# Cross-attention of a decoder layer: values of key tiles taken two by two in three of four head pairs, second half of the output projection one slot later

## The reference

```python
x = layernorm(x + attn(x))            # causal attention with squared features, 16 heads of 16
x = layernorm(x + xattn(x, ctx))      # 8 heads of 64:
#   q = x @ Wq ; k = ctx @ Wk ; v = ctx @ Wv
#   out = softmax(q k^T / 8) v ; out @ Wo + bo
x = layernorm(x + ffn(x))             # 8 experts, each token goes to its best 2
```

## Time and profile before

| | us |
|---|---|
| median of the timed runs | 1395.97 |
| the profiled execution's own time | 1389.87 |
| its span, first to last instruction | 1388.1 |
| cross-attention in it | 361 to 1106 |
| TensorE busy over the span | 1204.9 (87%) |
| VectorE / ScalarE / GpSimd busy | 769.4 / 587.1 / 681.5 |

### The profile page before, as it was taken

The page is one execution under the profiler, slowest core; times in us unless marked ns, Lnnn a source line. Parts: engine busy times, 40 slices in busy tenths (PEclk is TensorE's granted clock), DMA queues, the critical chain, the costliest instruction groups (busy, mean ns, idle before and its releaser), DMA issues. The chain is left out here.

```text
span 1388.1 us, 19049 instructions
## 1 busy us (share of the span) xinstructions
PE 1204.9 (87%) x6456; PEld 696.9 (50%) x6456; DVE 769.4 (55%) x1427; ACT 587.1 (42%) x1017; POOL 681.5 (49%) x601
## 2 busy tenths in 40 slices
PE   3567777875899999999999999999999799999990
PEld 3334544543455555555555555555555356666660
DVE  6575768655445574455683466655567343433325
ACT  3446555752344454344544444543544322222222
POOL 0123332442257776577777577685777821311112
PEclk8587989886899999999999999999999899999995
DMA  5490000010000010000010000000003531211104
GB/s 186 158 342 23 2 0 2 1 48 24 1 1 1 1 48 0 1 1 1 25 32 24 0 1 1 25 31 1 1 1 131 202 108 31 76 42 42 43 27 181
DMA packets 33132, 64.83 MB, mean 47 GB/s; under 512 B 4349, under 2 KB 22526, under 8 KB 32768
## 3 DMA queue, kind: packets, MB, share of 16 engines
q1 hardware_dynamic: 23328, 32.41, 7.3%
q10 hardware_dynamic: 6304, 22.76, 5.1%
q0 software_dynamic: 3408, 8.46, 1.7%
HBM read 53.06 MB, written 28.51 MB: 59 GB/s over the span
## 5 line engine op out<-in xcount | busy, mean ns | idle before, releaser
L671 POOL TENSOR_TENSOR acc<-acc,PX 128x1024 f32<-128x1024 f32 (+1 forms) x176 | 418.8, 2379 | 138.5 <-ACT PX L941 132.0
L941 ACT ACTIVATE PX<-PS 128x1024 f32<-128x1024 f32 (+1 forms) x208 | 212.4, 1026 | 269.3 <-PE PS L1759 262.9
L1407 DVE TENSOR_REDUCE mxp<-PS 128x2 f32<-128x804 f32 x256 | 241.8, 988 | 130.9 <-PE PS L1674 130.7
L1770 PE MATMUL PS<-PX,V 128*64 128x512 f32 (+1 forms) x832 | 222.6, 620 | 2.0 <-ACT O_raw L883 1.1
L609 POOL TENSOR_SCALAR_AFFINE_SELECT A<-A 128x128 f32<-128x128 f32 x256 | 85.4, 345 | 215.1 <-ACT A L822 211.8
L1828 PE MATMUL PS<-W,XBT 128*128 x312 | 150.6, 606 | 1.1 <-ACT XBT L973 0.8
L720 POOL DMA_INDIRECT Y<-yb,goal_u x39 | 38.3, 983 | 194.1 <-DVE yb L1473 175.0
L822 ACT ACTIVATE A<-PS 128x512 f32<-128x512 f32 (+3 forms) x256 | 97.3, 443 | 72.5 <-PE PS L1570 66.2
L1570 PE MATMUL PS<-qT,kT 128*128 128x512 f32 (+3 forms) x256 | 81.0, 401 | 36.4 <-ACT A L822 31.3
L1759 PEld LDWEIGHTS PS<-QH,KH 64*128 64x128 f32 (+1 forms) x416 | 38.3, 180 | 145.4 <-issue 87.5
L1759 PE MATMUL PS<-QH,KH 64*128 64x512 f32 (+1 forms) x416 | 102.9, 491 | 2.5 <-ACT PX L941 1.3
(11 more groups left out here) (275 smaller groups left out, 2111.7 us busy)
## 6 DMA issues: line engine op xcount, KB each, us to landing
W<-in_w SPq DMA_DIRECT2D x24, 512.0 KB, 5.1
XB<-XG ACTq DMA_DIRECT2D x39, 130.0 KB, 2.1
yl<-Y SPq DMA_DIRECT2D x8, 512.0 KB, 6.7
X<-in_x SPq DMA_DIRECT2D x1, 2048.0 KB, 12.0
out<-X SPq DMA_DIRECT2D x8, 256.0 KB, 2.1
xt_raw<-in_xt SPq DMA_DIRECT2D x3, 512.0 KB, 4.4
c_raw<-in_ctxt SPq DMA_DIRECT2D x6, 200.0 KB, 2.5
c_raw<-in_ctxt SPq DMA_DIRECT2D x12, 100.0 KB, 2.6
```

What stands on the lines that cost most here:

```text
L671: ins = pool.tensor_tensor(sums[0:r], sums[0:r], PX[0:r, (NL * p + t) % NP, :, :], ALU.add)
L941: act.activation(PX[0:r, u % NP, :, :], PS[0:r, score_buffer(u):score_buffer(u) + 2, :], ACT.Exp, scale=XD ** -0.5)\
L1407: dve.tensor_reduce(mxp[:, p % 2, :, v % NT, v // NT:v // NT + 1].rearrange("p a o -> p (a o)"), PS[:, k:k + 2, 0:BW], AX, ALU.max)\
L1770: mm = pe.matmul(PS[rows, 4, :], V[0:LROWS[j], j, P * p + XD * half:P * p + XD * half + XD], PX[0:LROWS[j], u % NP, half, :], start=(j == ...
```

## The change

For the pairs p = 1, 2, 3 a new table `VALUES_LATER` says in which slot the values of which tiles are taken: tiles 0 and 1 in slot 2, 2 and 3 in slot 4, 4 and 5 in slot 6, 6 and 7 in slot 8, 8 and 9 in slot 10, tile 10 in slot 11. Slots 1, 3, 5, 7 and 9 take none. Tiles 11 and 12 stay in slot 0 of the next pair, and pair 0 stays as it was. For p of 1 or more the second half of `wo` moves from slot 8 to slot 9, and the transposes that stood in slot 9 (`ft` 1 at p = 1, `xt` 0 at p = 2) move to slot 8.

```diff
-        ROUTING = {(1, 6): [("ft", 0)], (1, 9): [("ft", 1)], (1, 10): [("gate",), ("choose", 0)],
+        ROUTING = {(1, 6): [("ft", 0)], (1, 8): [("ft", 1)], (1, 10): [("gate",), ("choose", 0)],
...
-                if j in (7, 8):
-                    steps += [(ob, ("wo", op, j - 7))]
+                if j in (7, 9 if p >= 1 else 8):
+                    steps += [(ob, ("wo", op, 0 if j == 7 else 1))]
...
             if p == PAIRS - 2 and more:
-                steps += {6: [(1, ("xcopy",))], 9: [(1, ("xt", 0))], 10: [(1, ("xt", 1))], 11: [(1, ("ctx", 0))], 12: [(1, ("ctx", 1))]}.get(j, [])
+                steps += {6: [(1, ("xcopy",))], 8: [(1, ("xt", 0))], 10: [(1, ("xt", 1))], 11: [(1, ("ctx", 0))], 12: [(1, ("ctx", 1))]}.get(j, [])
...
+        VALUES_LATER = {2: [0, 1], 4: [2, 3], 6: [4, 5], 8: [6, 7], 10: [8, 9], 11: [10]}
...
+                        elif p >= 1:
+                            for t in VALUES_LATER.get(j, []):
+                                values_t(b, NL * p + t)
                         elif 1 <= j < NL - 1:
                             values_t(b, u - 1)
```

More of the change, by code:

```diff
@@ L310, in decoder_layer @@
                    (3, 9): [("scatter", 0)], (3, 10): [("scatter", 1)], (3, 11): [("scatter", 2)], (3, 12): [("scatter", 3)]}
-        LAST_ROUTING = {(1, 6): [("ft", 0)], (1, 9): [("ft", 1)], (1, 10): [("gate",), ("choose", 0)],
+        LAST_ROUTING = {(1, 6): [("ft", 0)], (1, 8): [("ft", 1)], (1, 10): [("gate",), ("choose", 0)],
                         (1, 11): [("choose", 1)], (1, 12): [("choose", 2)], (2, 0): [("choose", 3), ("choose", 4)],
```

## The result

| | before | changed |
|---|---|---|
| median of 16 runs each, us | 1396.44 (1392.26 to 1400.58) | 1390.43 (1384.48 to 1395.59) |
| ratio of the runs, 95% interval | | 0.996 (0.9946 to 0.9975) |
| profiled execution, us | 1389.87 | 1389.92 |
| its span, us | 1388.1 | 1388.0 |
| first transpose of the experts, us | 1105.82 | 1104.95 |

The change makes the kernel faster by 0.4%, 6.0 us of the medians; 1390.4 us was forecast. But the two profiled executions are equally long. The execution of before that was profiled was faster than all 16 timed ones, and the one of the changed kernel had bad luck in one place, which the second experiment shows. A single pair of traces gives a wrong answer on the sum here, and the right one on the parts.

A forecast was written before the change was run, and what follows sets the result against it. TensorE's own sequence of starts was taken as the bound. Terms -7.2 + 0.8 + 0.6 + 0.2 + 0.9 + 0.7 - 1.6 = -5.6 us took the median from 1395.97 to 1390.4 us, range 1383 to 1398.

The forecast's parts named there:

- the three places that were named: TensorE waits: step from pair 2 to 3, 2.50 us; slot 1 of pair 3, batch 0, 1.15; last pair's head output, 5.84.
- rivals 2 and 3: Short slots lose it again in small waits, 1395.4 us, chance 0.25; ScalarE copies delay their exponentials, 1407 us, chance 0.07.
- The price of a merge: Slots 3, 5, 7, 9 lose their group of values: 0.15 us each, 48 merges, -7.2 us; slot 1 saves nothing.
- The cover: Short slots of 2.61 and 2.39 us outlast the exponential's 2.31; only bank 7 waits, 0.07 us in slots 8 and 10, +0.8.
- Pair 3 of batch 0: Copy TR replaces slot 1's lost wait and VectorE is behind with the reciprocal; four merges come to nothing, +0.6 us.
- +0.8 + 0.6 + 0.2 for waits: Losses in us: bank 7 in slots 8 and 10; pair 3 of batch 0; pair 3 of batches 1 and 2.
- two merges of pair 2 and four of pair 3 lie in that shadow: Last batch, from slot 7 of pair 2: VectorE's routed slots set the head output, so these merges gain nothing, +0.9 us.
- The 5.84 us take the wait up: Last batch, slot 9 of pair 2: head-output wait absorbs `counts`' wait of at least 1.5 us; late maxima cost +0.7.
- The end, -1.6: End of the last pair: slot 10's scores start 2.0 us earlier, less 0.4 for slot 9's exponential; bounds 0 and -2.0.
- rival 1: Step from pair 2 to 3: the context split starts before GpSimd's sum, 1.7 us less in batches 0 to 2, 1385.3; chance 0.15.

The follow-up runs named there:

- the second experiment, after_again: The changed kernel run again without an edit, with a second trace: 1389.61 us, ratio 0.9965 to the kernel before.
- tile0_slot1: The changed kernel with tile 0 of the later pairs back in slot 1 and tile 1 alone in slot 2: 1384.87 us, ratio 0.9967 to before.
- values_only: The changed kernel without the moves of `wo` and the transposes, only values taken two by two: 1389.53 us, ratio 0.9963 to before.
- counts_later: The changed kernel with `counts` and plan 0 of the last batch in slot 10 of pair 2 instead of slot 9: 1387.34 us, ratio 0.9946 to before.

## Why the prediction was right

- **The bound.** Right in the main: the three places that were named are the long waits of TensorE after the change too. Some shorter ones were not named. In batch 0 the total of pair 3 waits 0.38 to 0.48 us for QL (0.55 before). The maxima of pair 3 of batches 1 and 2 wait 0.45 us for mxp in slot 10, as they did for 0.37 and 0.41 in slot 8. In the last pair, which has no maxima, the scores of slots 4 and 6 wait 1.12 us each for the exponential: the short slots there have nothing to cover it. These stand ahead of the long wait for the head output and cost nothing. The forecast had listed such waits as signs of rivals 2 and 3; the sums by pair show that neither came.
- **The price of a merge, 0.15 us, and none in slot 1.** Right: pairs of 1.86 us, and tile0_slot1 with 6.25 us against 6.24.
- **The cover.** Right to 0.01 us: 2.62 and 2.40 us of short slots, floor 2.31 (values_only), 0.08 us for bank 7 where 0.07 was put. The four slots 3 to 6 of pair 2 of batch 1 are shorter by 0.29 in sum, 0.3 was put.
- **Pair 3 of batch 0.** Slots 1 and 2 together 2.59 + 5.52 = 8.11 us against 8.20, slot 4 longer by 0.4 (4.90 against 4.48). The copy TR did take the place of the wait that went, and slot 4 waits for VectorE, which is behind with the reciprocal: its low half of the keys (L1425) ends at 515.67 us and the next key product starts at 515.73, 0.89 us after the maxima in place of 0.46. The pair gained 0.33 us where 0 was forecast. TensorE's timeline there in the changed kernel:

```profile
508.22 0.45 PE L1663 MATMUL PS<-Ch,WKh 128*128 128x402 f32 x1 [1.34 <-ACT TR L918]
```

- **Batches 0 to 2 and pair 1 of batch 3 without slot 0 of pair 3.** Forecast: 40 merges, -6.0, and +0.8 + 0.6 + 0.2 for waits, -4.4 us. The sums of after_again's slots against those of the first trace of before give -2.25 in pairs 1, -1.23 in pairs 2, -1.38 in pairs 3, together -4.9 us.
- **The step "two merges of pair 2 and four of pair 3 lie in that shadow", with VectorE as the one that must deliver.** Wrong for pair 2, right for pair 3. VectorE's 1.88 us were read as its own work, and were a wait for GpSimd's sum: the instruction takes 0.17. The chain into the last pair goes over GpSimd's last sum, so over TensorE's scores of slot 11; the head output ends 25.2 to 25.3 us after the pair's start in every kernel but those with moved scatters. "The 5.84 us take the wait up" was wrong with it: the 1.50 us of `counts` are paid in full. Pair 2 became longer by 0.8 us (after_again) or 4.0 (first trace), where -0.3 and +0.7 were put.
- **The end, -1.6.** Too large: from the head output to the experts -0.7 (15.4 against 16.2) and -1.1 us (15.0), and nothing in counts_later (16.1). The loads on ScalarE are issued 10.7 and 10.3 us after the head output in place of 11.4, so 0.7 and 1.1 us earlier against it where some 1.6 were put. The direction was right, but behind a wait of over 5 us slot 8 runs with the low clock (4.50 and 4.11 us for work that takes 2.99 in slot 4), and I had put it at full speed.

```profile
1100.25 2.48 ACTq L932 DMA_DIRECT2D XB<-XG  x3
```

- **Not in the sum: slot 0 of pair 3.** In the four traces of kernels with values in every slot it took 9.80, 8.77, 9.58 and 9.87 us in batch 1 and 8.37, 8.22, 8.34 and 8.48 in batch 2; in the six with merges and the context where it was, 8.74, 8.59, 8.48, 8.41, 8.21 and 6.96, and 8.26, 6.72, 8.28, 8.16, 8.01 and 8.21. Mean against mean that is 1.3 + 0.4 = 1.7 us. The wait is still there, so rival 1 did not come, but it is shorter in every trace with merges: 2.12 to 2.32 us against 2.50 to 2.54 in batch 1 and 1.88 to 2.08 against 2.27 to 2.29 in batch 2. That is 0.5 us of the 1.7; the rest is how long the clock is low behind it. This was seen, not tested.

So the nearness of 5.6 us to the 6.0 measured is in part luck. The last batch, from pair 2 on, came out worse than its terms by 0.8 us in after_again and by 4.3 in the first trace of the changed kernel. The rest came out better, by 0.5 us in the terms and by about 1.7 in slot 0 of pair 3, for which there was no term.

## What to carry to other kernels

Groups of matmuls of one shape belong together, but read what each group covers first: a slot's floor was the round trip of the scores' buffer, 2.31 us, and the merges paid only since each short slot kept 2.4 us of other work. When a step moves, look at what then stands directly behind it on the same bank: two steps back to back, `wo` and `counts`, cost more in one place than 6 merges gave. And follow a chain over each queue to the engine that feeds it: where two releasers end in the same tenth of a microsecond, as VectorE's routed slots and GpSimd's last sum did, compare their durations with those of the same instructions elsewhere. One of 1.88 us that takes 0.17 alone was held by the other.

## What the runs showed of the hardware

- A wait of 1.50 us before `counts` was followed by the low clock for about 6 us in one execution of a kernel and not in another, 3.2 us apart. The same kernel varies by several microseconds for that; one trace does not show what a wait costs.
- A change between the shapes 64*128, 128*64 and 128*128 costs 0.15 us for a group of values that is entered and left; total and values, both 128*64, cost nothing between them.
- Two VectorE subtractions in a row, each beside another GpSimd sum and ending 0.3 to 0.4 us behind it, took 2.75 and 2.63 us where 0.57 is their length alone. A VectorE multiplication of 128x8 values took 1.88 us beside such a sum and 0.17 without one.
- A load of 130 KB issued 1 us behind weight loads of 512 KB each landed after about 5 us, 2.1 us being its median. That the weights were the reason is not shown.
